# ViT encoder block on one core: key weighting moved to GpSimd, value copies to ScalarE, row maxima sent through DRAM into a spare row of the padded queries

## The reference, cut to what matters

```python
h = tok(x, W, b)                                   # 196 patches of 768 values -> 256
h = concatenate([cls_tok, h], axis=1)              # T = 197
xn = layernorm(h)
# per head (xh: 197 x 16), the weight pairs are multiplied together first
q = rms_norm(xh @ Wq, q_norm_w);  k = rms_norm(xh @ Wk, k_norm_w)
scores = (q . k + q_r . k_r) * 16 ** -0.5           # q_r = q @ W_QR.T, k_r = xh @ W_KR.T
attn = softmax(scores + causal)
h = h + (attn @ v) @ W_O.T
h = h + ffn(layernorm(h))                          # 3 cycles of a 4-layer net, a second pass
```

## Time and profile before

| what | value |
|---|---|
| runs shown | 4721.07 us median of 3 (4716.72 to 4723.11) |
| profiled execution | 4748.72 us, its span 4747.0 us |
| granted clock of PE, mean | 0.981 |
| busy share of the span | PE 93%, PEld 63%, DVE 79%, ACT 52%, POOL 23% |
| one step of the first pass | 24.9 us |
| first pass, about | 0 to 3291 us |

### The profile page before, as it was taken

The page is one execution under the profiler, slowest core; times in us unless marked ns, Lnnn a source line. Parts: engine busy times, 40 slices in busy tenths (PEclk is TensorE's granted clock), DMA queues, the critical chain, the costliest instruction groups (busy, mean ns, idle before and its releaser), DMA issues.

```text
span 4747.0 us, 83896 instructions
## 1 busy us (share of the span) xinstructions
PE 4412.8 (93%) x30223; PEld 2967.5 (63%) x30478; DVE 3729.9 (79%) x8990; ACT 2478.3 (52%) x5890; POOL 1097.6 (23%) x1936
## 2 busy tenths in 40 slices
PE   6999999999999999999999999997999999999998
PEld 4677777776776777777677777675444444444444
DVE  6888888888888888888888888885677777777776
ACT  3555555555555555555555555553444444444444
POOL 1333233333333332332333332332000000000000
PEclk9999999999999999999999999998999999999999
DMA  3343434333333433343333343332111111111111
GB/s 82 95 103 93 104 95 103 97 99 95 100 95 96 103 95 100 96 102 93 95 93 102 96 103 92 96 97 71 48 55 51 59 58 49 58 58 50 58 58 38
DMA packets 273568, 395.21 MB, mean 83 GB/s; under 512 B 23682, under 2 KB 223875, under 8 KB 273155
## 3 DMA queue, kind: packets, MB, share of 16 engines
q1 hardware_dynamic: 273154, 389.82, 31.1%
HBM read 130.45 MB, written 51.64 MB: 38 GB/s over the span
## 4 chain that ended last, share of the span: by engine, by line
PE 60%; DVE 28%; issue 6%; ACT 5%; DVEq 0%; DMA 0%; POOL 0%; SPq 0%; POOLq 0%
PE ps L1252 11%; PE ps L1008 10%; PE ps L1261 6%; PE ps L1096 5%; PE ps L1053 5%; DVE qkv L760 4%; PE ps L1270 4%; DVE qkv L769 3%; PE ps L1266 3%; PE ps L987 3%; DVE qkv L771 3%; DVE q L785 3%; PE ps L1068 2%; ACT kT L492 2%; DVE st L719 2%
## 5 line engine op out<-in xcount | busy, mean ns | idle before, releaser
L987 PE MATMUL ps<-w_tok,xb 128*128 128x256 f32 (+1 forms) x3072 | 827.9, 393 | 0.3 <-DVE small L704 0.3
L1252 PE MATMUL ps<-X,cn_w 128*128 128x394 f32 x1536 | 554.6, 504 | 0.0
L1096 PE MATMUL ps<-kZ,qT 128*69 128x396 f32 x1024 | 404.3, 444 | 161.1 <-DVE mx L812 159.0
L498 ACT ACTIVATE p<-ps 128x394 f32<-128x394 f32 x1024 | 454.9, 497 | 150.7 <-PE ps L1024 130.4
L439 POOL TENSOR_SCALAR_AFFINE_SELECT p<-p 128x512 f32<-128x512 f32 x512 | 358.4, 700 | 742.9 <-ACT p L498 735.3
L816 DVE TENSOR_REDUCE mx<-ps 69x2 f32<-69x396 f32 x1024 | 528.1, 555 | 0.0
L1018 PE MATMUL ps<-qZ,kT 128*128 128x396 f32 (+1 forms) x2048 | 508.1, 330 | 1.3 <-DVE att L805 1.2
L987 PEld LDWEIGHTS ps<-w_tok,xb 128*128 128x128 f32 (+1 forms) x3072 | 450.3, 165 | 81.0 <-issue 1.6
L1008 PE MATMUL ps<-w_qkv,hnT 128*128 128x512 f32 (+1 forms) x1024 | 494.8, 606 | 0.0
L453 POOL TENSOR_TENSOR h<-h,att 128x256 f32<-128x256 f32 (+1 forms) x256 | 181.0, 728 | 1248.8 <-DVE att L805 1248.8
L516 ACT ACTIVATE sq<-ps 128x256 f32<-128x256 f32 (+1 forms) x512 | 195.7, 382 | 510.9 <-PE ps L1008 510.7
(11 more groups left out here) (139 smaller groups left out, 9221.4 us busy)
## 6 DMA issues: line engine op xcount, KB each, us to landing
kZ<-kT SPq DMA_DIRECT2D x512, 198.0 KB, 3.5
qZ<-qT SPq DMA_DIRECT2D x256, 396.0 KB, 5.2
xb<-in_x SPq DMA_DIRECT2D x128, 588.0 KB, 6.6
h_scratch<-h SPq DMA_DIRECT2D x128, 128.0 KB
hl<-h_scratch SPq DMA_DIRECT2D x64, 256.0 KB
hk<-h_scratch SPq DMA_DIRECT2D x64, 256.0 KB
out<-hk SPq DMA_DIRECT2D x64, 256.0 KB
h_scratch<-h SPq DMA_DIRECT2D x128, 69.0 KB
```

Source lines behind the costliest of these rows:

```text
L498: s.activation(p0[:, i, 2 * jj:2 * jj + 2, :], ps[:, (b0, b1)[jj], 0:2 * TE].rearrange("p (a b) -> p a b", b=TE)[:, :, 0:T], ACT.Exp).then ...
L987: mm = t_.matmul(ps[:M, W[t], 0:D], xb[:, par, k, t * P:t * P + M], w_tok[:, k, :], start=k == 0, stop=k == KT - 1)
L1096: t_.matmul(bank, qT[:, j, P:T], kZ[:, :, j, :], start=True, stop=False)
L1252: mm = t_.matmul(ps[:, 4 * c + mt, 0:N2], cn_w1[:, f, mt * P:mt * P + P], X[:, c, state(cyc), f, :], start=f == 0, stop=f == FT - 1)
```

## The change

Five edits, all in the first pass:

1. `less_max`, `pair_sel`, `parity` and `mxP` go. `mxT_copy` makes one copy of the 16 x 197 maxima into `mxT`; SP sends it to DRAM (`mx_scratch`), waits for that, and loads the rows back into row 48 of each 64-row half of `qZ` (one DMA for the even and one for the odd heads). The fourth slot of `k2` now holds a 1 in its first channel, so row 48 of `kT` is 1 and `products` subtracts the maximum by itself. `scoresT(o, 0)` waits for the rows (`mx_loaded`).
2. The two operations L769 and L771 on k move from DVE to POOL (`k_weighted`), ahead of `norm` and the `select` calls.
3. `ctx_copy` (L790) moves from DVE to ACT.
4. The small operations of the RMS norm are done for both t at once (`rms`, `rms_small`).
5. PE does `embed_part(1, 0)` ahead of the first `scoresT`, and the others one place earlier; the orders of DVE, ACT and POOL change as the diff shows.

```diff
+            def max_rows(m):
+                sp.wait_ge(mxT_ready, m + 1)
+                sp.dma_start(mx_dram[m % 2], mxT[:].bitcast(F32)).then_inc(mx_stored, 16)
+                sp.wait_ge(mx_stored, m * 16 + 16)
+                sp.wait_ge(qZ_loaded, m * 32 + 32)
+                for c in range(2):
+                    row = c * P // 2 + 3 * HD
+                    sp.dma_start(qZ[row:row + 1, c, :, 0:T].bitcast(F32),
+                                 mx_dram[m % 2:m % 2 + 1, c:H:2, :]).then_inc(mx_loaded, 16)
+
             def step(n, r):
                 par = 1 - r % 2
+                if there(n - 2):
+                    max_rows(n - 2)
...
+            def k_weighted(m, r, t):
+
+                M = TS[t]
+                n = m * 2 + t + 1
+                k = qkv[:M, r, t, K, :, 0:HD]
+                wk = wk_row[:M, :].rearrange("p (o d) -> p o d", o=1).to_broadcast([M, H, HD])
+                wait(qk_normed, n)
+                g.tensor_tensor(k, k, wk, ALU.mult).then_inc(kw_done, 1)
+                pool.wait_ge(kw_done, n)
+                g.tensor_tensor(k, k, qkv[:M, r, t, R, :, 0:HD], ALU.add).then_inc(k_ready, 1)
+
...
                     residual(n - 3, (r + 1) % 4)
+                if there(n):
+                    k_weighted(n, r, 0)
+                    k_weighted(n, r, 1)
+                if there(n + 1):
+                    norm(n + 1, 0)
                 if there(n - 2):
                     select(n - 2, 0)
                     select(n - 2, 1)
-                if there(n + 1):
-                    norm(n + 1, 0)
-                if there(n - 2):
                     select(n - 2, 2)
...
                 if there(n - 2):
                     exps(n - 2, 0)
-                    exps(n - 2, 1)
                 if there(n):
                     q_high_part(n, r, 0)
                 if there(n - 2):
-                    exps(n - 2, 2)
+                    exps(n - 2, 1)
                 if there(n):
                     q_high_part(n, r, 1)
                 if there(n - 2):
+                    exps(n - 2, 2)
                     exps(n - 2, 3)
                 if there(n + 1):
                     hnT_copy(n + 1, 0)
+                if there(n - 2):
+                    ctx_copy(n - 2, 0, ctx0_ready)
+                if there(n + 1):
                     hnT_copy(n + 1, 1)
+                if there(n - 2):
+                    ctx_copy(n - 2, 1, ctx1_ready)
...
                 dve.wait_ge(mx_transposed, m + 1)
-                for c in range(2):
-                    v.tensor_scalar(mxP[:H, c, 0:T], ps[:H, MB, 0:T], parity[:H, c:c + 1], None, ALU.mult)\
-                     .then_inc(mxP_ready, 1)
+                if m:
+                    dve.wait_ge(mx_stored, m * 16)
+                v.tensor_copy(mxT[:], ps[:H, MB, 0:T]).then_inc(mxT_ready, 1)
...
-                def less_max(b, x_, j, keys, queries, last):
-
+                def products(b, x_, j, keys, queries, last):
                     M, N = keys.stop - keys.start, queries.stop - queries.start
                     mm = t_.matmul(ps[:M, b, x_ * 2 * N:x_ * 2 * N + 2 * N].rearrange("p (a b) -> p a b", b=N),
-                                   pair_sel[:, j:j + 1].to_broadcast([P, M]), mxP[:, :, queries],
-                                   start=False, stop=last)
+                                   kT[:, par, j, keys], qZ[:, :, j, queries], start=x_ == 0, stop=last)
...
+                if i == 0:
+                    pe.wait_ge(mx_loaded, m * 32 + 32)
...
+                embed_part(1, 0)
                 if there(o):
                     if there(m):
                         pe.wait_ge(kT_ready, n * 4)
                         pe.wait_ge(qT_ready, n * 4 - 3)
                     pe.wait_ge(qZ_loaded, n * 32 - 32)
                     scoresT(o, r % 2, 0)
-                embed_part(1, 0)
+                embed_part(1, 1)
```

More of the change, by code:

```diff
@@ L290, in build @@
         ]
-        N_CV = 21
+        N_CV = 20
         N_W = 16 * (len(small_w) + 1)
@@ L517, in qkv_copy, with rms @@
                 copy(qkv[:M, r, t, :, 8 * f:8 * f + 8, 0:HD], bank).then_inc(qkv_ready, 1)
[L519 to L527, removed]
+            def rms(m):
+                act.wait_ge(ss_ready, m * 2 + 2)
+                s.activation(ls[:], ss[:], ACT.Ln, bias=rms_eps[:, 0:1], scale=1.0 / HD).then_inc(ls_ready, 1)
+                act.wait_ge(ls_ready, m + 1)
+                s.activation(rs[:], ls[:], ACT.Exp, scale=-0.5).then_inc(rs_ready, 1)
             def q_high_part(m, r, t):
@@ L534, in q_high_part, with ctx_copy @@
                 copy(q2[:M, t, :, 0:3:2, :], x_.to_broadcast([M, H, 2, HD])).then_inc(q_high, 1)
+            def ctx_copy(m, jj, done):
+                act.wait_ge(pv_done, m * 2 + jj + 1)
+                copy(ctxT[:, 2 * jj:2 * jj + 2, :], ps[:, W[jj], 0:N2].rearrange("p (a b) -> p a b", b=T))\
+                    .then_inc(done, 1)
             def kT_copy(m, par, b):
@@ L550, in step @@
                 if there(n):
-                    rms(n, 0)
+                    rms(n)
                 if there(n - 1):
@@ L556, in step @@
                     qT_copy(n - 1, 1)
-                if there(n):
-                    rms(n, 1)
                 if there(n - 1):
@@ L739, in rms_sum, with rms_small @@
                  .then_inc(ss_ready, 1)
+            def rms_small(m):
+                dve.wait_ge(ss_ready, m * 2 + 2)
+                v.tensor_scalar(xh[:], ss[:], -0.5 / HD, -0.5 * RMS_EPS, ALU.mult, ALU.add).then_inc(xh_ready, 1)
+                dve.wait_ge(rs_ready, m + 1)
+                v.tensor_tensor(y2[:], rs[:], rs[:], ALU.mult).then_inc(y2_ready, 1)
+                dve.wait_ge(xh_ready, m + 1)
+                dve.wait_ge(y2_ready, m + 1)
+                v.tensor_tensor(y2[:], y2[:], xh[:], ALU.mult).then_inc(y2x_ready, 1)
+                dve.wait_ge(y2x_ready, m + 1)
+                v.scalar_tensor_tensor(rms[:], y2[:], 1.5, rs[:], ALU.add, ALU.mult).then_inc(rms_ready, 1)
             def rms_mul(m, r_, t):
                 M = TS[t]
[L743 to L757, removed]
+                dve.wait_ge(rms_ready, m + 1)
                 qk = qkv[:M, r_, t, Q:K + 1, :, 0:HD]
@@ L1034, in scoresT @@
                         pe.wait_ge(e_done, n - 5 + x_)
[L1035 to L1039, removed]
+                    products(*first[x_], True)
                 if i > 1:
@@ L1042, in scoresT @@
                 for x_ in range(2):
-                    products(*second[x_])
-                for x_ in range(2):
-                    less_max(*second[x_], x_ == 1)
+                    products(*second[x_], x_ == 1)
             def pv(m, r, jj):
@@ L1156, in step @@
                     scoresT(o, r % 2, 1)
-                embed_part(1, 1)
+                embed_part(1, 2)
                 if there(o):
                     scoresT(o, r % 2, 2)
-                embed_part(1, 2)
-                if there(o):
                     scoresT(o, r % 2, 3)
```

51 lines of the change are left out of this document (19 added, 32 removed).

## The result

The changed kernel takes 4818.83 us (median of 4; 4797.46 to 4842.73) against 4720.84 us: a ratio of 1.021, with a 95% interval of 1.0154 to 1.0266. It is slower by about 98 us where 165 us less were forecast. The profiled execution took 4805.85 us. Ratios leave out executions that lie over 1.5% above the fastest of their kernel, where enough others are left.

What follows compares the result with a forecast made beforehand. PE bounds the first-pass step, with a 1.33 us gap released by DVE's first maxima; releasing PE 1.29 us earlier over 128 images saves 165 us from 4721, about 4555 us. Forecast 4500 to 4610, range 4430 to 4690 us.

Steps and rivals of the forecast that it cites:

- The sum of the step: First pass, one image: the step goes from 24.93 to 23.64 us, 1.29 less.
- what I had counted: PE's scoresT without less_max: 0.48 us saved per scoresT, about 1.95 us per step.
- The term of DVE and POOL: Ahead of the first maxima: operations laid in turn, k at 0.73 us each on POOL; PE released at 13.95, not 15.24.
- the second case below: DVE and POOL in the first pass: k operations run beside DVE, 282 us saved, 4440 us; chance 0.20.
- rival 1: DVE and POOL hardly meet in the first pass: step 22.7 us, 282 saved, 4440 us; chance 0.20.
- PE's pace, unchanged: PE from pv(o, 1) to the end of the step: 7.51 us as before.
- The two gaps that I forecast: PE waits about 0.95 us on exps 2 before scores(m, 0), about 0.9 us on first maxima before L1096.
- rival 2: DVE and POOL meet more, selects late: step 24.1 to 24.9 us, 4615 to 4720 us; chance 0.14.
- Rivals 3 and 4: Slower: POOL's k, norm, select chain, 4960 us, chance 0.07; late DMA rows at first product, 5060 us, chance 0.06.

Runs made afterwards that it cites:

- q_low_late: The changed kernel with the DVE call q_low_part(n, 1) moved from ahead of the embedding to behind maxima(n-1, 0); 4503.54 us, ratio 0.9516.
- fill_half: The changed kernel with 11 small idle-filling matmuls on PE ahead of the wait on the first maxima only; 4617.92 us, ratio 0.9785.
- k_on_dve: The changed kernel with the weighting and sum of k back on DVE (edit 2 undone); 4691.12 us, ratio 0.9951.
- q_low_embed: q_low_late with PE's old interleaving of embed_part(1, *) and scoresT (edit 5 undone as well); 4516.47 us, ratio 0.9575.

## Why the prediction was wrong

**The sum of the step was right to 0.57 us.** Measured at full clock, from 130.35: PE at `scores(m, 0)` at 11.06 (forecast 11.0), at `hn_transpose` 12.12 (12.1), at the wait on the maxima released at 14.52 (13.95), `pv(o, 1)` at 16.70 (16.13), the end at 24.21 (23.64). `less_max` saved what I had counted, and the tail is the 7.51 us of before.

**The term of DVE and POOL was mis-sized, and the 0.57 us is the rest of two larger errors.** The four operations on k took 0.96, 0.74, 0.68 and 0.80 us for the 0.73 each forecast, but they were not laid in turn as I had them: the first one began after the first scaling and not after the second, and DVE had done its low part of q for t = 0 by 10.0, a whole microsecond ahead of my 11.0. Then it stood 0.47 us for the norm on POOL, whose two small operations took 0.68 and 1.11 us. What I did not price is the low part of q for t = 1 beside the selects, 1.68 instead of 0.4 us. It set the first maxima at 13.8 instead of 13.2; in `q_low_late`, without it, they start at 12.2 and PE goes on at about 12.9. That the sum comes within 0.57 us is thus in part luck. The change at full clock is worth about 75 us instead of 165. What the Trainium skill says of the pair ("SBUF — State Buffer", who interferes with whom) pointed the right way, and the price here, 1.3 us, was higher than one instruction's length. The prediction calls the sum without it "the second case below"; the case meant is its rival 1.

**The step that failed is "PE's pace, unchanged".** I counted what followed a gap at the pace of before and took no price for what a gap does to the clock. The mean clock of 0.981 stood in the table of before and the steps with a low clock were in its trace; I had read only windows at 1.00. The two gaps that I forecast, 0.95 us each, would have cost little: `fill_half`, with 0.87 and 0.94 us, has no long step. The 1.48 that came was not harmless, and it costs some 200 us. So, as far as `fill_half` may stand for it, an error of 0.57 us in one start time turned a gain into a loss.

**The rivals.** Rival 1 (DVE and POOL hardly meet) and rival 2 (they meet more) were about the size of the step. Its length at full clock, 24.2 us, lies at the start of rival 2, though the selects were not late: the last one ends at 16.1, as forecast, and `pv(o, 1)` starts at 16.7. Rivals 3 and 4 named slower, but by causes that did not occur: the operations on k took at most 0.97 us, and the rows of the maxima were loaded early: in the step from 130.35 the store is issued at 130.14, the two loads from 131.56 (t = 1.2), which is earlier than the 2.2 I had given. `ctx_copy` on ACT cost nothing that shows; it was not tried by itself, and neither was edit 4. No rival had the clock.

## What to carry to other kernels

Where PE is near its limit, a cut in its work makes it wait, and in this kernel waits of over a microsecond also cost time after they have ended, because the granted clock falls behind them. So look up the mean clock before costing an edit, and test with idle-filling matmuls, which tell the price of the clock in one run. Take work off the engine that releases PE first, or split the wait in two. And do not put a VectorE instruction with two SBUF inputs beside a row of GpSimd operations on the way to what everybody waits for; here such an instruction took four times as long.

## What was unexpected of the hardware

- The dependence on the gaps is steep: 0.94 us (with 0.87) costs next to nothing, 1.33 us alone (before) about 29 us over the run, 1.48 us (with 0.85) some 200. The largest gap is not the whole of it: 1.04 us with 0.85 and 0.47 beside it (`k_on_dve`) has no fewer long steps than the 1.33, and `q_low_embed`, with 0.55 us in most steps and 0.9 in some, still has 6. The low steps come in rows: 18 times 27.3 us in a row and then several of 24.2, with the same gaps in both. Why the same gaps meet the low clock in one stretch and not in the next was not tried.
- One VectorE instruction with two SBUF inputs stood while three POOL selects went ahead of it (1.68 us for 0.41, at mean 1674 ns over 104 steps). It did not get its turn after the first of them. The Trainium skill, "SBUF — State Buffer", in the section on who interferes with whom, has the exclusion of the two; that the loser can lose several times in a row is what the rows here add. The layer norm's power on POOL took 1.10 us beside DVE for the 0.72 of before.
- The way out to DRAM is short for 12 KB: 1.4 us from the issue of the store to its landing, the median in the list of DMA issues.
